# Messages that overflow from one span of relations into the next, in the second direction of a graph layer

## What is computed

```
H_all = jnp.einsum('rod,nd->rno', W_rel, input) + b_rel[:, None, :]     # 16 relations: 8 each way
msg_to_heads = H_all[rel, tails]
msg_to_tails = H_all[rel + R, heads]
agg = segment_sum(msg_to_heads, heads, N) + segment_sum(msg_to_tails, tails, N)
x = x + relu(input @ W_self.T + b_self + agg)
```

## Time and profile before

| | us |
|---|---|
| median of 3 runs | 719.96 (719.37 to 720.86) |
| the profiled execution | 720.36 |
| its span, first to last instruction | 718.6 |
| TensorE busy | 692.0 (96%) |
| VectorE busy | 618.6 (86%) |
| ScalarE busy | 508.3 (71%) |
| GpSimd busy | 306.5 (43%) |
| mean granted TensorE clock | 0.992 of full |
| one copy of a product out of PSUM (L693), mean | 0.58 |

### The profile page before, as it was taken

How to read it: one execution, slowest core, us unless ns; L and a number is a source line. 1 busy time by engine, 2 the same in 40 slices (tenths; PEclk the granted TensorE clock), 3 DMA queues, 4 the chain that set the end, 5 groups by cost and what they waited for, 6 DMA issues and landing times. The chain is left out here.

```text
span 718.6 us, 10605 instructions
## 1 busy us (share of the span) xinstructions
PE 692.0 (96%) x3216; PEld 545.8 (76%) x3216; DVE 618.6 (86%) x1208; ACT 508.3 (71%) x722; POOL 306.5 (43%) x279
## 2 busy tenths in 40 slices
PE   5999999999999999999997989999999999999996
PEld 4777777777777777787755868788888888888884
DVE  8699979998999777777676889999999999999982
ACT  5646467766777777777556678888787888888881
POOL 3000048785877777777770033222221333333301
PEclk9999999999999999999998999999999999999998
DMA  8357579987988999988668979999999999999952
GB/s 252 107 171 264 166 220 318 307 279 243 303 280 284 326 307 305 304 282 247 202 202 289 358 232 390 407 406 401 405 369 405 378 375 383 363 390 368 355 200 30
DMA packets 60972, 213.33 MB, mean 297 GB/s; under 512 B 9485, under 2 KB 9882, under 8 KB 47870
## 3 DMA queue, kind: packets, MB, share of 16 engines
q1 hardware_dynamic: 41534, 154.43, 57.2%
q0 software_dynamic: 19392, 58.35, 27.7%
HBM read 184.46 MB, written 28.29 MB: 296 GB/s over the span
## 5 line engine op out<-in xcount | busy, mean ns | idle before, releaser
L409 POOL DMA_INDIRECT rows_sb<-h_dram,row_of x190 | 217.6, 1145 | 152.8 <-DVE row_of L554 89.4
L564 DVE TENSOR_TENSOR rows_lo<-rows_sb,rows_hi 128x512 fp32r<-128x512 f32 x175 | 120.0, 686 | 38.9 <-ACT rows_hi L706 38.4
L706 ACT CAST rows_hi<-rows_sb 128x512 fp32r<-128x512 f32 x175 | 106.3, 619 | 55.5 <-DMA rows_sb<-h_dram,row_of 51.3
L848 PE MATMUL p_h<-g_hi_sb,xt_hi_whole 128*125 128x512 f32 x320 | 129.0, 403 | 0.6 <-DVE xt_lo_whole L487 0.5
L849 PE MATMUL p_h<-g_lo_sb,xt_hi_whole 128*125 128x512 f32 x320 | 127.1, 397 | 0.0
L850 PE MATMUL p_h<-g_hi_sb,xt_lo_whole 128*125 128x512 f32 x320 | 127.0, 397 | 0.0
L1224 POOL DMA_INDIRECT tokens<-token_dram,rows_of_tokens x15 | 19.7, 1310 | 175.8 <-ACT rows_of_tokens L1530 135.4
L693 ACT COPY h_whole<-p_h 125x512 f32<-125x512 f32 x80 | 46.7, 583 | 51.6 <-PE p_h L850 46.6
L1278 DVE TENSOR_TENSOR u_lo_sb<-stage_up,u_hi_sb 128x2048 fp32r<-128x2048 f32 x34 | 76.4, 2285 | 0.9
L1278 DVE TENSOR_TENSOR d_lo_sb<-stage_down,d_hi_sb 128x2048 fp32r<-128x2048 f32 x32 | 71.9, 2286 | 3.8 <-ACT d_hi_sb L1515 3.8
L884 PE MATMUL p_sum<-rows_hi,seg_hot 128*125 128x512 f32 x175 | 71.4, 408 | 2.8 <-DVE rows_lo L564 2.5
(11 more groups left out here) (298 smaller groups left out, 1312.1 us busy)
## 6 DMA issues: line engine op xcount, KB each, us to landing
stage_up<-in_L_ffn_up_w SPq DMA_DIRECT2D x34, 1024.0 KB, 8.9
stage_gate<-in_L_ffn_gate_w SPq DMA_DIRECT2D x32, 1024.0 KB, 8.9
stage_down<-in_L_ffn_down_w SPq DMA_DIRECT2D x32, 1024.0 KB, 8.7
h_dram<-h_whole SPq DMA_DIRECT2D x80, 256.0 KB, 4.0
stage_up<-in_L_gnn_W_rel SPq DMA_DIRECT2D x64, 256.0 KB, 5.1
x_whole<-in_biases SPq DMA_DIRECT2D x16, 256.0 KB, 6.5
rows_sb<-h_dram,row_of POOLq DMA_INDIRECT x190, 5.2
stage_gate<-in_L_ffn_down_w SPq DMA_DIRECT2D x2, 1024.0 KB, 10.1
```

The lines of the kernel that those rows point to most:

```text
L409: q.indirect_dma_start(rows_sb[:, b % ROWS], None, h_dram[0:1 + made(n) * P], bass.IndirectOffsetOnAxis(ap=row_of[:, b:b + 1].bitcast(U32) ...
L564: v.tensor_tensor(rows_lo[:, b % PARTS], rows_sb[:, b % ROWS], rows_hi[:, b % PARTS].bitcast(F32), ALU.subtract).then_inc(part_lo, 1)
L706: s.copy(rows_hi[:, b % PARTS], rows_sb[:, b % ROWS]).then_inc(part_hi, 1)
L848: m.matmul(o, xt_hi[:, dc, at], wt_hi_sb[:, 1 - j % 2, dc], start=(by_matmul and dc == 0), stop=False, skip_group_check=True)
```

## The change

In the second direction the spans have 6, 5, 4 and 3 blocks a tile, 18 in place of 20, 180 blocks in all. A tile's messages in that direction now stand in one row of places through all four spans: where a span's messages don't fit in its own blocks, the rest stands at the beginning of the next span's, whose own messages come behind it. So the later spans need a **beginning** for each tile: the larger of where the blocks of the span begin and of where the messages before it end. `spans_begin` works these out from the counts in a chain of three steps and writes them, less `HALF`, as a further row of `totals` (row 96), which the ranks' matmuls add through `columns_before`. TensorE forms the counts straight after product 2, and the ranks of the second direction stand behind product 3, after a wait for `totals_ready` 5. The list's columns are ordered by tile, `column_of` finds a block's. If a tile has more than 18 blocks hold, the stage runs again.

```diff
-SPANS = ((0, 0, 4, 9), (0, 4, 8, 9), (1, 0, 3, 7), (1, 3, 5, 5), (1, 5, 7, 5), (1, 7, 8, 3))
+SPANS = ((0, 0, 4, 9), (0, 4, 8, 9), (1, 0, 3, 6), (1, 3, 5, 5), (1, 5, 7, 4), (1, 7, 8, 3))
+IN_TILE = [sum(c for d, _, _, c in SPANS if d == way) for way in range(2)]
+SLOT_OF = [P * sum(c for way, _, _, c in SPANS[:n] if way == d) for n, (d, _, _, _) in enumerate(SPANS)]
+HELD = P * SPANS[0][3]
+HALF = P * IN_TILE[1] // 2
+EXTRA = 96
...
-            totals = sb("totals", [EC, BUCKETS], F16, g)
-            crow = sb("crow", [1, BUCKETS], F32, g)
-            per_block = sb("per_block", [1, 2, BUCKETS], F32, g)
+            totals = sb("totals", [EXTRA + 1, BUCKETS], F16, g)
+            columns_before = sb("columns_before", [EXTRA + 1, EC], F16, g)
+            crow = sb("crow", [EXTRA + 1, BUCKETS], F32, g)
+            ends = sb("ends", [EXTRA + 1, 3, T], F32, g)
...
+            column_of = [IN_DIR[0] * d + t * IN_TILE[d] + SLOT_OF[n] // P + k
+                         for n, (d, _, _, c) in enumerate(SPANS) for t in range(T) for k in range(c)]
...
-                                         bass.IndirectOffsetOnAxis(ap=row_of[:, b:b + 1].bitcast(U32), axis=0)
+                                         bass.IndirectOffsetOnAxis(ap=row_of[:, column_of[b]:column_of[b] + 1].bitcast(U32), axis=0)
...
+                    if d:
+                        then(v.scalar_tensor_tensor(bucket[:, d], listed_before[:], float(BUCKETS), bucket[:, d], ALU.mult, ALU.add))
...
+                def spans_begin():
+
+                    dve.wait_ge(counts_full, 1)
+                    then(v.tensor_copy(crow[:], p_counts))
+                    count = [crow[:, n * T:(n + 1) * T] for n in range(len(SPANS))]
+                    dve.wait_ge(edge_consts, 1)
+                    for k in range(3):
+                        n = 3 + k
+                        filled = count[2] if k == 0 else ends[:, k - 1]
+                        v.tensor_scalar(totals[EXTRA:EXTRA + 1, n * T:(n + 1) * T], filled[EXTRA:EXTRA + 1], float(SLOT_OF[n]), float(HALF),
+                                        ALU.max, ALU.subtract).then_inc(totals_ready, 1)
+                        then(v.scalar_tensor_tensor(ends[:, k], filled, float(SLOT_OF[n]), count[n], ALU.max, ALU.add))
...
                     if i == 3:
+                        spans_begin()
+                    if i == 4:
                         ranks(1)
-                        dve.wait_ge(counts_full, 1)
-                        v.tensor_copy(crow[:], p_counts)
...
                     if i == 2:
                         pe.wait_ge(totals_ready, 2)
+                        m.matmul(p_counts, ones16[0:EC, 0:EXTRA + 1], totals[0:EC], start=True, stop=True).then_inc(counts_full, 1)
+                        turn_x(4)
+                    if i == 3:
+                        pe.wait_ge(totals_ready, 5)
                         ranks(1)
-                        m.matmul(p_counts, ones16[0:EC, 0:1], totals[:], start=True, stop=True).then_inc(counts_full, 1)
-                        turn_x(4)
```

More of the change, by code:

```diff
@@ L30 @@
 ROUND = 3.0 * 2 ** 22
-SPANS = ((0, 0, 4, 9), (0, 4, 8, 9), (1, 0, 3, 7), (1, 3, 5, 5), (1, 5, 7, 5), (1, 7, 8, 3))
+SPANS = ((0, 0, 4, 9), (0, 4, 8, 9), (1, 0, 3, 6), (1, 3, 5, 5), (1, 5, 7, 4), (1, 7, 8, 3))
 NTH = [n - [s[0] for s in SPANS].index(d) for n, (d, _, _, _) in enumerate(SPANS)]
 BLOCKS = sum(T * c for _, _, _, c in SPANS)
-IN_DIR = [sum(T * c for d, _, _, c in SPANS if d == way) for way in range(2)]
+IN_TILE = [sum(c for d, _, _, c in SPANS if d == way) for way in range(2)]
+IN_DIR = [T * c for c in IN_TILE]
+SLOT_OF = [P * sum(c for way, _, _, c in SPANS[:n] if way == d) for n, (d, _, _, _) in enumerate(SPANS)]
+HELD = P * SPANS[0][3]
+HALF = P * IN_TILE[1] // 2
+EXTRA = 96
 BUCKETS = T * len(SPANS)
@@ L379, in then @@
                     pool.wait_ge(pool_steps, done)
[L381 to L385, removed]
+                then(q.memset(columns_before[64:EXTRA + 1], 1.0))
+                q.affine_select(out=columns_before[0:EC], in_=ones[0:EC, 0:EC], compare_op=ALU.is_gt, fill=0.0, base=0,
+                                pattern=[[1, EC]], channel_multiplier=-1).then_inc(edge_consts, 1)
                 q.memset(zero_rows, 0.0).then_inc(route_consts, 1)
[L387 to L390, removed]
                 q.tensor_copy(block_iota[:], iota_i[0:EP, 1:1 + max(IN_DIR)])
@@ L472, in told_of @@
-                    then(v.scalar_tensor_tensor(first_block[:, d], e_first[:, d], 1 / P, first_block[:, d], ALU.mult, ALU.add))
+                        v.tensor_scalar(held_before[:], trip[:], float(HELD), None, ALU.mult)
+                    v.tensor_scalar(first_block[:, d], e_tile[:, d], float(IN_TILE[d]), 1.0, ALU.mult, ALU.add)
+                    v.tensor_scalar(e_row[:], e_seg[:, 1 - d], 1.0, None, ALU.add)
+                    then(v.scalar_tensor_tensor(e_in[:, d], e_tile[:, d], -float(TP), e_seg[:, d], ALU.mult, ALU.add))
@@ L524, in places @@
                     place, here, nth = place_in[:, d], temp[:, 0, d], temp[:, 1, d]
-                    then(v.scalar_tensor_tensor(place, place, BIG, held_before[:, d], ALU.subtract, ALU.subtract))
-                    v.tensor_tensor(here, place, held[:, d], ALU.is_lt)
+                    if d == 0:
+                        then(v.tensor_scalar(place, place, BIG, held_before[0:EP, 0:1], ALU.subtract, ALU.subtract))
+                    else:
+                        then(v.tensor_scalar(place, place, BIG - HALF, None, ALU.subtract))
+                    v.tensor_scalar(here, place, float(P * IN_TILE[1] if d else HELD), None, ALU.is_lt)
                     then(v.tensor_scalar(nth, place, (P - 1) / 2, 1 / P, ALU.subtract, ALU.mult))
@@ L531, in places @@
                     v.scalar_tensor_tensor(lane[:, d], nth, -float(P), place, ALU.mult, ALU.add)
-                    then(v.scalar_tensor_tensor(nth, nth, 1.0, first_block[:, d], ALU.add, ALU.add))
+                    then(v.tensor_tensor(nth, nth, first_block[:, d], ALU.add))
+                    if d:
+                        v.tensor_tensor(listed_before[:], listed_before[:], here, ALU.max)
                     then(v.tensor_tensor(block_at[:, d], nth, here, ALU.mult))
@@ L813, in ranks @@
                 def ranks(k):
-                    _, n, past = PARTS_OF[k]
+                    d, n, past = PARTS_OF[k]
+                    rows, past_columns = (EXTRA + 1, columns_before) if d else (EC, before)
                     if k:
@@ L822, in ranks @@
                             i = m.matmul(p_ranks[0:EP, s - n, b * EC:(b + 1) * EC],
-                                         totals[:, T * s + b:T * s + b + 1].to_broadcast([EC, EP]), before[0:EC, 0:EC],
+                                         totals[0:rows, T * s + b:T * s + b + 1].to_broadcast([rows, EP]), past_columns[0:rows, 0:EC],
                                          start=False, stop=(b == T - 1))
```

54 lines of the change are left out of this document (24 added, 30 removed).

## The result

The kernel after takes 712.85 us (median of 4 runs, 711.7 to 713.61), the kernel before 719.66 us beside it (718.1 to 720.86). The ratio is 0.9905 with a 95% interval of 0.9879 to 0.9931. In a later comparison on one chip it was 0.9934 (0.9908 to 0.9959), with medians 3.6 us apart. The change makes the kernel faster by some 0.7 to 1.0%; forecast were 715.9 us, 0.6%.

The account below looks back on a forecast made before the run. TensorE was taken to bound the relation and expert stages, with GpSimd's gather queue late in the tail. Terms - 4.7 - 0.7 - 3.9 - 1.4 + 5.1 + 1.5 = - 4.1 us gave 715.9 us from the median; range 712.5 to 718.7.

Parts of the forecast that it names:

- rival (a): At the start, waiting for the beginnings costs 4.0 us or less and the clock doesn't fall: 713.3 or below; chance 0.14.
- Blocks: Second direction, ten blocks fewer, five between the last products and five in the tail: 20 matmuls less on TensorE, 4.7 us.
- Waits for gathers in the tail: Behind the last product, TensorE's waits of 3.9 and 1.4 us for late gathers both go.
- the four terms: Gains forecast from matmuls 4.7, lists 0.7, and waits for gathers 3.9 and 1.4 us.
- Rival (c): GpSimd's gather queue still sets the relation stage's end and the kernel is slower, such as 722.8 us; chance 0.05.
- Lists: The second direction's 85 list matmuls have 180 columns in place of 200, saving 0.7 us on TensorE.
- Where the ranks stand: At the start, TensorE waits for VectorE's beginnings, so product 4 begins at 39.3 in place of 34.24: 5.1 us lost.
- The clock: TensorE's waits at the start may drop it to 1.2 GHz: loss between 0 and 3 us, taken as 1.5.
- Rival (d): Messages don't fit in one pass and the whole stage runs twice, over 1050 us; chance under 0.01.

Follow-up runs that it names:

- the blocks alone: The kernel before with 6, 5, 4, 3 blocks a tile and one pass forced, without the overflow, leaving out messages that don't fit: 708.33 us against 718.30.
- the cut matmuls: The kernel before with all 190 gathers, but one two-column matmul in place of two of 512 for ten blocks: 719.47 us against 718.30.
- the early counts: The kernel after with counts formed straight behind product 1 and VectorE's chain in its idle time ahead of x's fourth tile: 707.87 us, 708.05 when repeated.
- With 20 blocks: The kernel after with 7, 5, 5, 3 blocks a tile in the second direction, keeping overflow and late ranks: 721.45 us against 718.30 before.
- the second profile: The kernel after, unchanged, profiled once more; its wait for the beginnings was 3.09 us.
- the filler: The kernel after with ten matmuls of 425 columns, results unread, in TensorE's wait ahead of the counts: 715.24 us beside 714.52 for the kernel after.

## Why the prediction was right, and by how much it was off

The time lies in the range, near its lower end, and the direction is right. The sum was 2.7 us too small against the profiled execution (4.1 forecast, 6.75 measured); the later comparison's medians, 3.6 us apart, would make it right. The 712.85 us fall where the prediction had put its rival (a), 713.3 or below, but not for that rival's reason: the loss at the start was not 4.0 or less. By its steps:

- **Blocks**, 4.7 us of matmuls: right as a term. The plan behaved as read, with a gap of 3.25 us between products 77 and 78 and of 2.79 to product 79, for 4.18 and 4.20 before.
- **Waits for gathers in the tail**, 3.9 + 1.4 us: both went; the blocks alone gave 10.0 us for the 10.7 of the four terms, and the cut matmuls gave nothing in the tail while the queue stood. Block 145's gather went at 322.97, forecast 324.2, the last at 370.16, forecast 370.2. That the second agrees so well is luck: the last matmul of product 74 began at 317.85, so the product ended over 1 us before the forecast's 319.6, and the 34 steps behind it took 1.388 us each in place of 1.352. Rival (c) fell.
- **Lists**, 0.7 us: right in size between products 30 and 54 (0.73), half wrong in kind, as 0.36 of it is a wait for VectorE.
- **Where the ranks stand**, 5.1 us: measured 5.3 us, or 5.0 counted from product 3, with the wait for the beginnings and the one ahead of the turn where they were said to be. That TensorE never gets it back was right as well, as the early counts showed, for a kernel with 18 blocks. With 20 blocks the tail took up 2.6 us in the one pair of profiles, and the medians show nothing of it.
- **The clock**, 1.5 us between 0 and 3: in the profiled execution it was 0, since the clock fell ahead of the wait; it was 3.0 in the second profile and 1.6 with the filler. Whether 1.5 was fair for the median isn't shown. The rule of the Trainium skill that I had set against the change, that waits between bursts put the clock to half rate ("TensorE: Matmul & The Clock Gate", on HAM oscillation), holds here, and already for waits shorter than those it tells of: in all five profiles with these waits the granted clock fell to 0.50 in one of them or behind it, in three of them behind the wait of 1.8 us. But the full 3 us were paid in one profile only.
- **Missing**: 1.1 us at the first blocks, from VectorE's shorter telling of the second direction (0.3 to 1.0 us over the profiles with the old one). The prediction has no term for it. It counted the telling of the first direction alone, and the sentence nearest to it puts VectorE's other savings beside TensorE's products, where they "cost nothing". That holds only where nobody waits for VectorE; the first gathers do. A further 0.6 us at product 53 is not explained.
- **Rival (d)** fell: the stage ran once. Its counts can't be right as written, since the five add up to 10706 messages and there are 10625 edges. Counted again from the reference's inputs, the tiles have 2198, 2109, 2077, 2154 and 2087 messages in the second direction, and with the places left free ahead of later spans the fullest ends at 2230 of 2304.

In the profiled executions the sum with these in place is - 4.7 - 0.7 - 5.3 + 5.3 + 0 - 1.1 - 0.6 = - 7.1, which is the difference of the spans (718.6 and 711.5). Two small things cancel in it: the tail and the boundary behind it gained some 0.7 us more than their terms (the wait ahead of the expert stage is 2.04 in place of 2.47 us), and the beginning of the expert stage gave 0.8 us back.

## What to carry to other kernels

Where one queue is late by a little, taking an item out of it is worth the item's own time on the bound engine and the wait behind it; taking the bound engine's part alone brought nothing in the tail here. A value that a full engine waits for belongs where the engine that makes it stands idle: the chain of seven small operations here cost 5 us behind the places and nothing 9 us earlier, and the version with the early counts beats both kernels, at 708 us. A short wait on TensorE also has a price that one profile doesn't show: the clock fell in or behind one of the waits in all five profiles, and what it cost, 0 to 3.0 us, hung on which.

## What the runs showed of the hardware

- A wait of 1.82 us on TensorE, in the kernel after, was followed by a fall of the granted clock to 0.50 while the next product was running; in another execution of the same kernel the same wait, 1.83 us, was not, and the one of 3.09 us behind it was.
- A wait of 2.16 us ahead of the last gather's matmuls, with the matmuls cut, was followed by 0.50 from 384 to 393; behind one of 1.44 us at the same place in the kernel before the clock stayed at 1.00 until 389.
- A gather of 128 rows costs GpSimd 1.13 to 1.15 us on average in all eleven profiles (1.145 before, 1.149 after), and in the tail their distance was 1.25 us at best.
